# Second attention: early scores ahead of the turned maxima, wider ones products, and the second copy of the maxima on GpSimd

## The chip, the cores and the metric

The kernel runs on one core of one Trainium2 chip. The metric is the device time of one execution in microseconds (us), taken as the median of several runs. The engines are TensorE (PE, its weight loads are shown apart as PEld), VectorE (DVE), ScalarE (ACT), GpSimd (POOL) and SyncE (SP), which here only issues transfers.

## The reference, cut to what matters

The program is two transformer layers. The change touches only the attention of the second one: batch 8, sequence 256, 32 heads of 16 dimensions, causal, float32.

```python
x0, x1 = (xr[..., 0], xr[..., 1])           # rotary, pairs of dimensions
o0 = x0 * c - x1 * s
o1 = x0 * s + x1 * c
...
scores = jnp.einsum('bqhd,bkhd->bhqk', q, k) * scale
scores = jnp.where(causal[None, None], scores, jnp.finfo(scores.dtype).min)
probs = jax.nn.softmax(scores, axis=-1)
out = jnp.einsum('bhqk,bkhd->bqhd', probs, v).reshape(b, s, d)
return out @ wo
```

## The kernel before, in words

The work of this attention is cut into 64 units of four heads each (8 per batch). Queries and keys of a unit come from DRAM as stacks of 52 rows: 4 rows for the negated maximum and 3 times 16 rows for a split of each operand into parts. A unit holds four heads as two halves (row groups 0 to 63 and 64 to 127 of the array) by two slots. The 256 queries and 256 keys are two blocks of 128.

For each unit the kernel computes the scores twice. The first time queries are on the partitions (`scores_early` for query block 0, `scores_late` for query block 1, both on top of a causal mask that `put_masks` writes by a product): from these VectorE takes the negated maximum of every query (`maxima`, one reduction per query block). TensorE turns these maxima from columns to rows (`turn_max`), into the front of PSUM bank 0. ScalarE copies the rows into the first four rows of the queries' stack, for the first half (`negated`, L2062), and again for the second half (`negated_again`, L2067). Then TensorE computes the scores a second time, now with keys on the partitions and with the maxima already subtracted, because they are rows of the stack (`shifted_near` for key block 0, `shifted_far` for key block 1). ScalarE takes the exponential (`exponentials`, L2087: 1024 columns, then 512), GpSimd zeroes what the causal mask leaves out in the diagonal blocks (`cut`), and `values` multiplies with the values and with a block of ones, which yields the sums of the rows. The ones products use, for queries of the second block, the sum of both key blocks' probabilities, which GpSimd has added before (`add_blocks`, L2120). VectorE takes the reciprocal of the sums (L2029) and multiplies (L2032), one block of 128 queries of a pair of units in each step. ScalarE and GpSimd split that into two parts for the last product (L2078, L2126).

The engines are programs of their own, written out by hand; semaphores order them. No scheduler moves anything. All run a loop over steps; in step v TensorE turns the maxima of unit v+1, computes the shifted scores of v, the early and late scores of v+2, and the values of v-1. Four slots hold the stacks; SyncE loads a unit's stack into its slot after the shifted scores of the unit four before it (`load_unit`, four transfers). TensorE executes in order, so each wait holds up all that stands behind it.

PSUM places matter for the waits: the early scores (`s0`) lie in the first half of banks 2 and 3, the shifted scores of key block 1 (`t1`) in the second half of the same two banks. The late scores (`s1`) fill banks 0 and 1, so they overwrite the turned maxima in bank 0: `scores_late` has to wait until ScalarE has copied these (`m_out`).

In the last steps of the stage (from `TAIL` on) each engine also does side work for the output projection, for VectorE an extra subtraction per step (L2492).

Of the kernel before, what the change touches and what calls it, by code (L numbers as in the profile page):

```python
# [21 lines left out]
P = 128  # L22
# [1891 lines left out]
def attention1(nc, io, keep, ctx):  # L1914
# [35 lines left out]
    both = [nc.alloc_sbuf_tensor_at(f"f_both{s}", [P, HU, P], F32, offset=keep.both_at + s * HU * P * 4) for s in range(2)]  # L1950
# [14 lines left out]
    m_out = sem("f_m_out")  # L1965
    t_done = sem("f_t_done")
    p_exp = sem("f_p_exp")
    p_cut = sem("f_p_cut")
    p_both = sem("f_p_both")
# [49 lines left out]
    def vector(dve, side):  # L2019
        def maxima(u, first):  # L2020
            for t, sc in ((0, s0), (1, s1)):
                dve.wait_ge(s_done, 4 * u + 2 * t + 2)
                nc.vector.tensor_reduce(neg_max[first][:, t].rearrange("p (e i) -> p e i", e=2), sc, AX, ALU.max, negate=True).then_inc(smax, 1)  # L2023
# [10 lines left out]
        def step(v, slot, at):  # L2034
            if at < U - 2:
                maxima(v + 2, slot % 2)
# [27 lines left out]
    def negated_again(act, u, slot):  # L2064

        act.wait_ge(m_out, 2 * u + 1)
        nc.scalar.activation(q[slot][64:64 + HU], f32(q[slot][0:HU]), ACT.Identity).then_inc(m_out, 1)  # L2067
# [5 lines left out]
    def scalar(act, side):  # L2073
# [16 lines left out]
        def step(v, slot, at):  # L2090
# [4 lines left out]
            if 0 <= at < U - 1:  # L2095
                negated_again(act, v + 1, (slot + 1) % NS)
# [11 lines left out]
    def gpsimd(pool):  # L2108
# [8 lines left out]
        def add_blocks(u, slot):  # L2117

            pool.wait_ge(p_cut, 2 * u + 2)
            nc.gpsimd.tensor_tensor(both[slot % 2][:], prob0[slot % 2][:, :, P:S], prob1[slot % 2][:], ALU.add).then_inc(p_both, 1)  # L2120
# [7 lines left out]
        def step(v, slot, at):  # L2128
            if 0 <= at < U:
                cut(v, slot)  # L2130
                add_blocks(v, slot)
            if 6 <= at and not slot % 2:
                low((v - 6) // 2)
# [20 lines left out]
    def scores_late(pe, u, slot, first=False):  # L2154

        if not first:
            pe.wait_ge(m_out, 2 * u - 1)
# [35 lines left out]
    def tensor(pe, side):  # L2193
# [20 lines left out]
        def values(u, slot):  # L2214
# [11 lines left out]
            pe.wait_ge(p_both, u + 1)  # L2226
            for p, c, cols in ((prob0[par][:, :, 0:P], 0, slice(0, P)), (both[par], 1, slice(P, S))):
# [5 lines left out]
        def step(v, slot, at):  # L2233
            if 0 <= at < U - 1:
                turn_max(pe, v + 1, (slot + 1) % 2, at)
            if 0 <= at < U:
                pe.wait_ge(m_out, 2 * v + 2)
                if at > 0:
# [3 lines left out]
                if at < U - 2:  # L2242
                    put_masks(0, False)
            if 0 <= at < U - 2:
                scores_early(pe, v + 2, (slot + 2) % NS)
# [23 lines left out]
def output1(nc, io, keep, ctx, out):  # L2269
# [76 lines left out]
    zeroed = sem("g_zeroed")  # L2346
    hi_done, lo_done = sem("g_hi_done"), sem("g_lo_done")
# [567 lines left out]
```

## Time and profile before

| | |
|---|---|
| median of 3 runs | 1948.7 us (1943.15, 1949.42, 1948.7) |
| the profiled execution | 1943.6 us, of which the span is 1941.9 us |
| TensorE, VectorE, ScalarE, GpSimd busy | 95%, 78%, 47%, 47% of the span |
| units of the second attention, first and last turned maxima | 1562.2 to 1791.5 us |
| TensorE's clock granted over the whole span | 0.984 |

The profile gives times from the start of the span. The second attention takes about an eighth of it; what is before it (the first attention, its output projection, the first layer's low-rank part, and the second layer's queries, keys and values) and behind it (output projection and the experts) is not touched. In the rows below a line is a group of like instructions; in a timeline its first number is its start, its second how long it lasted until the last one's end, and the bracket says how long the engine had been idle before it, and what released it.

### The profile page before, as it was taken

To read this page: it belongs to the slowest core of one execution; us is meant where nothing else is said; L and a number is where in the kernel's file an instruction comes from. 1 tells how busy PE (TensorE), PEld (TensorE's weight loads), DVE (VectorE), ACT (ScalarE), POOL (GpSimd) and SP (SyncE) were. 2 spreads that over 40 slices of the span, in tenths; PEclk is the share of its full clock that TensorE was granted. 3 is DMA by queue.
4 is the path that set the end of the run, shared out by engine and by line. 5 is a ranking of instruction groups with operands and counts; after the bars stand their busy time and mean duration, and the time that the engine had idled before them with its cause. 6 is when DMAs were issued, how large, how long until landed. Compare 5 with 4: busy or idle time off the path is not lost.

```text
span 1941.9 us, 38168 instructions
## 1 busy us (share of the span) xinstructions
PE 1853.3 (95%) x12760; PEld 1540.6 (79%) x12760; DVE 1506.6 (78%) x2385; ACT 919.5 (47%) x2297; POOL 907.3 (47%) x872
## 2 busy tenths in 40 slices
PE   8999988999999999999999999998999988998997
PEld 3688867888888888888888888886798966666786
DVE  2577747778888888888888888888788658889887
ACT  1233324444444444444444444454555457888433
POOL 0033354444444444444444444354377557888111
PEclk9999998999999999999999999998999989999999
DMA  9577751111111111111111111231277776554121
GB/s 341 168 231 245 249 166 41 50 49 49 49 50 46 43 41 48 49 49 49 49 49 49 44 42 43 93 96 52 87 233 233 219 223 202 168 168 127 39 65 60
DMA packets 201847, 211.39 MB, mean 109 GB/s; under 512 B 19082, under 2 KB 172682, under 8 KB 200748
## 3 DMA queue, kind: packets, MB, share of 16 engines
q1 hardware_dynamic: 200836, 209.53, 34.8%
q8 instruction: 47, 0.77, 0.2%
q10 hardware_dynamic: 936, 0.85, 0.1%
q14 instruction: 28, 0.23, 0.0%
HBM read 128.40 MB, written 73.53 MB: 104 GB/s over the span
## 4 chain that ended last, share of the span: by engine, by line
PE 68%; issue 13%; DVE 10%; POOL 4%; SPq 3%; DMA 2%; ACT 1%; DVEq 0%; POOLq 0%; ACTq 0%
PE ps L1066 18%; PE ps L1027 17%; PE ps L1040 7%; PE ps L1055 5%; PE ps L1078 4%; DVE f_neg_max L2023 4%; PE ps L1050 3%; SPq L1338 2%; POOL k_rot L574 2%; PE ps L2603 2%; PE ps L2639 2%; PE ps L1839 2%; PE ps L2197 2%; PE ps L2176 1%; PE ps L1849 1%
## 5 line engine op out<-in xcount | busy, mean ns | idle before, releaser
L1066 PE MATMUL ps<-wo,ot 128*128 (+1 forms) x1536 | 389.1, 402 | 0.0
L1066 PEld LDWEIGHTS ps<-wo,ot 128*128 128x128 f32 x1536 | 283.1, 191 | 58.8
L821 ACT ACTIVATE prob<-ps,neg_max 128x128 f32<-128x128 f32 (+1 forms) x512 | 208.6, 421 | 131.2 <-DVE neg_max L902 109.2
L1027 PE MATMUL ps<-ht_hi,wq 128*128 (+1 forms) x1024 | 255.5, 392 | 5.5 <-DVE q_swap L895 5.5
L981 POOL TENSOR_TENSOR q_rot<-q_rot,q_swap 128x512 f32<-128x512 f32 x128 | 164.7, 1288 | 180.0 <-DVE q_swap L895 175.4
L828 ACT ACTIVATE pt<-ps 128x512 fp32r<-128x512 f32 x192 | 108.0, 597 | 283.7 <-PE ps L1078 283.6
L1027 PEld LDWEIGHTS ps<-ht_hi,wq 128*128 128x128 f32 x1024 | 193.2, 189 | 47.8 <-issue 5.9
L975 POOL TENSOR_TENSOR prob<-prob,inv_sum 128x512 f32<-128x512 f32 x64 | 66.6, 1041 | 292.2 <-DVE inv_sum L911 292.2
L574 POOL TENSOR_TENSOR k_rot<-k_rot,k_swap 128x512 f32<-128x512 f32 x32 | 60.2, 1883 | 193.7 <-DVE k_swap L479 193.7
L877 DVE TENSOR_TENSOR ot<-ps,ot 128x512 fp32r<-128x512 f32 x128 | 88.3, 691 | 76.6 <-ACT ot L838 76.4
L1040 PE MATMUL ps<-pt,vv 128*128 128x512 f32 x576 | 144.4, 395 | 3.4 <-issue 2.9
L2023 DVE TENSOR_REDUCE f_neg_max<-ps 128x4 f32<-128x512 f32 (+1 forms) x128 | 116.8, 952 | 33.2 <-PE ps L2142 25.5
L1027 PE MATMUL ps<-ht_lo,wq 128*128 (+1 forms) x512 | 137.8, 391 | 0.0
L1040 PEld LDWEIGHTS ps<-pt,vv 128*128 128x128 f32 x576 | 108.9, 190 | 29.2 <-issue 3.8
L838 ACT ACTIVATE ot<-ps 128x512 fp32r<-128x512 f32 x128 | 76.8, 600 | 106.1 <-PE ps L1040 106.1
L872 DVE TENSOR_TENSOR pt<-ps,pt 128x512 fp32r<-128x512 f32 x192 | 120.9, 684 | 6.0 <-ACT pt L828 4.0
L885 DVE TENSOR_TENSOR x_stream<-ps,x_stream 128x512 f32 (+1 forms) x112 | 77.4, 691 | 58.6 <-PE ps L1066 56.3
L2087 ACT ACTIVATE f_prob<-ps 128x1024 f32<-128x1024 f32 (+1 forms) x128 | 102.0, 798 | 28.6 <-DVE f_neg_max L2023 26.5
L1027 PEld LDWEIGHTS ps<-ht_lo,wq 128*128 128x128 f32 x512 | 96.7, 189 | 20.2
L1078 PE MATMUL ps<-ident,prob 128*128 128x128 f32 x768 | 98.5, 279 | 12.9 <-POOL prob L975 11.4
L1078 PEld LDWEIGHTS ps<-ident,prob 128*128 128x128 f32 x768 | 90.1, 144 | 23.0 <-POOL prob L975 12.5
L1055 PE MATMUL ps<-kk,q 128*128 128x256 f32 x768 | 107.4, 289 | 0.0
(247 smaller groups left out, 4125.5 us busy)
## 6 DMA issues: line engine op xcount, KB each, us to landing
stack_dram<-e_part SPq DMA_DIRECT2D x192, 128.0 KB, 2.4
v_dram<-v_part SPq DMA_DIRECT2D x32, 512.0 KB, 5.9
k_dram<-k_part SPq DMA_DIRECT2D x64, 256.0 KB, 2.5
kk<-k_dram SPq DMA_DIRECT2D x128, 128.0 KB, 2.1
vv<-v_dram SPq DMA_DIRECT2D x128, 128.0 KB, 2.1
f_q<-stack_dram SPq DMA_DIRECT2D x124, 104.0 KB
f_k<-stack_dram SPq DMA_DIRECT2D x124, 104.0 KB
wmod<-in_wmod SPq DMA_DIRECT2D x12, 1024.0 KB, 11.9
```

What stands on the lines that cost most here:

```text
L574: nc.gpsimd.tensor_tensor(krot[g % 2][:], krot[g % 2][:], kswap[g % 2][:], ALU.add).then_inc(k_rot, 1)
L821: nc.scalar.activation(p[:, h], sc[:, h], ACT.Exp, bias=neg_max[:, t, h:h + 1], accum_out=row_sum[:, t, h:h + 1]).then_inc(p_exp, 1)
L828: nc.scalar.activation(pt[0][:, j], ps_s[:, j], ACT.Identity).then_inc(t_hi, 1)
L872: nc.vector.tensor_tensor(pt[1][:, j], ps_s[:, j], f32(pt[0][:, j]), ALU.subtract).then_inc(t_lo, 1)
L981: nc.gpsimd.tensor_tensor(qrot[:, at, j], qrot[:, at, j], qswap[j][:], ALU.add).then_inc(q_add, 1)
L1027: mm = nc.tensor.matmul(ps_q[j][:], w[:, at:at + HD0], r[:, bass.ds(b, 2), k], start=(n == 0), stop=(n == len(passes) - 1))
L1040: mm = nc.tensor.matmul(ps_o[j][:], a[:, k], p[:, blk], start=(n == 0), stop=(n == len(passes) - 1))
L1055: mm = nc.tensor.matmul(s1[:, h], a[:, slot(r, h // 2), h % 2], b[:], start=(n == 0), stop=(n == 2))
L1066: mm = nc.tensor.matmul(ps_y[j][:], o[:, j, h * P:(h + 1) * P], w[:, bass.ds(at + h * D, D)], start=(n == 0), stop=(n == len(passes) - 1))
L1078: mm = nc.tensor.transpose(ps_s[:, blk, h * P:(h + 1) * P], src, keep.ident[:])
L2023: nc.vector.tensor_reduce(neg_max[first][:, t].rearrange("p (e i) -> p e i", e=2), sc, AX, ALU.max, negate=True).then_inc(smax, 1)
L2087: nc.scalar.activation(p[slot % 2][:].rearrange("p (e i) s -> p e i s", e=2), sc, ACT.Exp, scale=SCALE1).then_inc(p_exp, 1)
```

## The change

Three things are changed. First, on TensorE, in step v the masks and early scores of unit v+2 are moved from behind the shifted scores of v to the very front of the step, ahead of the turned maxima of v+1. They now wait for VectorE's first reduction of unit v+1 and for both exponentials of unit v-1; the mask product now starts its accumulation group. VectorE's reduction of those scores now also waits for the shifted scores of unit v. Second, the ones products stream the probabilities themselves: key block 0 with all 256 queries and key block 1 with the second 128, in place of 128 and 128 columns; GpSimd's addition is gone. Third, the second copy of the maxima is made by GpSimd, ahead of its two cuts, and not by ScalarE behind the exponentials; it has a semaphore of its own, `m_again`, and `m_out` now counts one per unit.

```diff
@@ vector: maxima
-        def maxima(u, first):
+        def maxima(u, first, at):
+            if at >= 0:
+                dve.wait_ge(t_done, 4 * u - 4)
             for t, sc in ((0, s0), (1, s1)):
@@ the second copy, now a function of gpsimd
-        act.wait_ge(m_out, 2 * u + 1)
-        nc.scalar.activation(q[slot][64:64 + HU], f32(q[slot][0:HU]), ACT.Identity).then_inc(m_out, 1)
+            pool.wait_ge(m_out, u + 1)
+            nc.gpsimd.nop(nofuse=True)
+            nc.gpsimd.tensor_copy(q[slot][64:64 + HU], f32(q[slot][0:HU])).then_inc(m_again, 1)
@@ scalar: step
-            if 0 <= at < U - 1:
-                negated_again(act, v + 1, (slot + 1) % NS)
@@ gpsimd
-        def add_blocks(u, slot):
-            pool.wait_ge(p_cut, 2 * u + 2)
-            nc.gpsimd.tensor_tensor(both[slot % 2][:], prob0[slot % 2][:, :, P:S], prob1[slot % 2][:], ALU.add).then_inc(p_both, 1)
...
         def step(v, slot, at):
+            if 0 <= at < U - 1:
+                if at == 0:
+                    pool.wait_ge(keep.row_zeroed, 2)
+                if at >= 1:
+                    pool.wait_ge(p_cut, 2 * v)
+                if at >= 6 and slot % 2:
+                    pool.wait_ge(o_split, (v - 5) // 2)
+                negated_again(v + 1, (slot + 1) % NS)
+                pool.wait_ge(m_again, v + 2)
             if 0 <= at < U:
                 cut(v, slot)
-                add_blocks(v, slot)
@@ tensor: scores_late
-            pe.wait_ge(m_out, 2 * u - 1)
+            pe.wait_ge(m_out, u)
@@ tensor: values
-            pe.wait_ge(p_both, u + 1)
-            for p, c, cols in ((prob0[par][:, :, 0:P], 0, slice(0, P)), (both[par], 1, slice(P, S))):
+            for p, c, cols in ((prob0[par], 0, slice(0, S)), (prob1[par], 1, slice(P, S))):
@@ tensor: step
+            if 0 <= at < U - 2:
+                pe.wait_ge(smax, 2 * v + 3)
+                if at > 0:
+                    pe.wait_ge(p_exp, 2 * v)
+                put_masks(0, True)
+                scores_early(pe, v + 2, (slot + 2) % NS)
             if 0 <= at < U - 1:
                 turn_max(pe, v + 1, (slot + 1) % 2, at)
             if 0 <= at < U:
-                pe.wait_ge(m_out, 2 * v + 2)
-                if at > 0:
+                pe.wait_ge(m_again, v + 1)
+                if at >= U - 2:
                     pe.wait_ge(p_exp, 2 * v)
                 shifted_near(v, slot)
                 shifted_far(v, slot)
-                if at < U - 2:
-                    put_masks(0, False)
-            if 0 <= at < U - 2:
-                scores_early(pe, v + 2, (slot + 2) % NS)
             if 0 <= at < U - 2:
                 scores_late(pe, v + 2, (slot + 2) % NS)
```

How TensorE's order changes in one step is seen in its instructions. Before, one step of TensorE reads as follows: turned maxima (`f_neg_max`), shifted scores (`ps<-f_q,f_k`), mask (`halves_b`), early scores (128 columns), mask, late scores (256 columns), values (`f_v`) and ones (`f_ones`).

```order
L2176 MATMUL ps<-ident,f_neg_max_196 4x128 x2
L2197 MATMUL ps<-f_q_50,f_k_54 128x256 x4
L2197 MATMUL ps<-f_q_50,f_k_54 128x128 x4
L2151 MATMUL ps<-halves_b 128x256 x4
L2142 MATMUL ps<-f_k_56,f_q_52 128x128 x4
L2151 MATMUL ps<-halves_b 128x2x128 x4
L2142 MATMUL ps<-f_k_56,f_q_52 128x256 x4
L2224 MATMUL ps<-f_prob_187,f_v_59 32x256 x4
L2224 MATMUL ps<-f_prob_189,f_v_59 32x128 x4
L2229 MATMUL ps<-f_prob_187,f_ones 32x128 x4
L2229 MATMUL ps<-f_both_191,f_ones 32x128 x4
```

The same step in the changed kernel, from its first instruction to its last:

```order
L2159 MATMUL ps<-halves_b 128x256 x4
L2150 MATMUL ps<-f_k_56,f_q_52 128x128 x4
L2184 MATMUL ps<-ident,f_neg_max_194 4x128 x2
L2205 MATMUL ps<-f_q_50,f_k_54 128x256 x4
L2205 MATMUL ps<-f_q_50,f_k_54 128x128 x4
L2159 MATMUL ps<-halves_b 128x2x128 x4
L2150 MATMUL ps<-f_k_56,f_q_52 128x256 x4
L2232 MATMUL ps<-f_prob_187,f_v_59 32x256 x4
L2232 MATMUL ps<-f_prob_189,f_v_59 32x128 x4
L2236 MATMUL ps<-f_prob_187,f_ones 32x256 x4
L2236 MATMUL ps<-f_prob_189,f_ones 32x128 x4
```

A mask and the early scores have gone from behind the shifted scores to the front; between the turned maxima and the second mask only the shifted scores are left; the first group of ones products has 256 columns in place of 128.

GpSimd, two steps before: two cuts of the probabilities and the addition.

```order
L2114 AFFINE_SELECT f_prob_187<-f_prob_187 128x4x128
L2114 AFFINE_SELECT f_prob_189<-f_prob_189 128x512
L2120 TENSOR_TENSOR f_both_191<-f_prob_187,f_prob_189 128x512
L2114 AFFINE_SELECT f_prob_186<-f_prob_186 128x4x128
L2114 AFFINE_SELECT f_prob_188<-f_prob_188 128x512
L2120 TENSOR_TENSOR f_both_190<-f_prob_186,f_prob_188 128x512
```

The same two steps in the changed kernel:

```order
L2120 CAST f_q_52<-f_q_52 4x512
L2113 AFFINE_SELECT f_prob_187<-f_prob_187 128x4x128
L2113 AFFINE_SELECT f_prob_189<-f_prob_189 128x512
L2120 CAST f_q_53<-f_q_53 4x512
L2113 AFFINE_SELECT f_prob_186<-f_prob_186 128x4x128
L2113 AFFINE_SELECT f_prob_188<-f_prob_188 128x512
```

The copy of the maxima (`CAST`) stands ahead of the cuts, and the additions are gone.

## Rows read from the trace of the kernel before

**Rows 1.** Windows of two stretches: span, busy by engine, clock, DMA share, GB/s

```profile
1589.02:1767.55 178.53, 163.17 (x3020) 119.28 (x3016) 154.01 (x208) 149.61 (x234) 147.57 (x181) 0.99 0.60 180
1771.53:1791.37 19.84, 16.11 (x291) 11.45 (x292) 19.67 (x26) 16.80 (x28) 16.04 (x19) 1.00 0.40 121
```

**Rows 2.** Waits in the first of these stretches: total us, times, longest us

```profile
PEld ps L2176 <- DVE f_neg_max L2023: 25.7, 50, 0.5
DVE f_neg_max L2023 <- PE ps L2142: 13.5, 41, 2.1
...
PEld ps L2142 <- DMA f_k<-stack_dram: 3.5, 2, 1.9
```

**Rows 3.** Chain that ended last between 1600 and 1780 us, by line

```profile
by line: DVE f_neg_max L2023 36.0%; PE ps L2197 15.8%; issue 15.0%; PE ps L2176 9.8%; PE ps L2142 6.2%; PE ps L2151 6.1%; DMA f_k<-stack_dram 5.2%; DVE f_inv_sum L2029 1.9%; DVE g_lo L2492 1.7%; SPq L1905 0.8%; PE ps L2224 0.6%; DVEq L2030 
```

**Rows 4.** Timeline of TensorE's weight loads over one unit: start us, us

```profile
1690.69 0.09 PEld L2176 LDWEIGHTS ps<-ident,f_neg_max 128*4 128x4 f32 x2 [0.51 <-DVE f_neg_max L2023]
1691.00 0.54 PEld L2197 LDWEIGHTS ps<-f_q,f_k 52*128 52x128 f32 x8 [0.22 <-ACT f_q L2067]
1691.52 0.12 PEld L2151 LDWEIGHTS ps<-halves_b 64*128 64x128 bf16 x4
1691.64 0.31 PEld L2142 LDWEIGHTS ps<-f_k,f_q 52*128 52x128 f32 x4
1691.93 0.12 PEld L2151 LDWEIGHTS ps<-halves_b 64*128 64x128 bf16 x4
1692.06 0.30 PEld L2142 LDWEIGHTS ps<-f_k,f_q 52*128 52x128 f32 x4
1692.50 0.59 PEld L2224 LDWEIGHTS ps<-f_prob,f_v 128*32 128x32 f32 x16
1693.07 0.24 PEld L2229 LDWEIGHTS ps<-f_prob,f_ones 128*32 128x32 f32 x8
1693.29 0.24 PEld L2229 LDWEIGHTS ps<-f_both,f_ones 128*32 128x32 f32 x8
1694.04 0.09 PEld L2176 LDWEIGHTS ps<-ident,f_neg_max 128*4 128x4 f32 x2 [0.51 <-DVE f_neg_max L2023]
```

**Rows 5.** The same unit on ScalarE, VectorE and SyncE's queue

```profile
1690.55 0.95 DVE L2029 RECIPROCAL f_inv_sum<-ps 128x128 f32<-128x128 f32 x1
...
1691.11 0.59 ACT L2062 ACTIVATE f_q<-ps 4x512 fp32r<-4x512 f32 x1 [0.32 <-PE ps L2176]
...
1691.60 1.00 ACT L2087 ACTIVATE f_prob<-ps 128x1024 f32<-128x1024 f32 x1
...
1691.65 0.29 DVE L2032 TENSOR_TENSOR turned_raw<-ps,f_inv_sum 128x128 f32 x1
...
1692.16 1.82 DVE L2023 TENSOR_REDUCE f_neg_max<-ps 128x4 f32<-128x512 f32 x2 [0.22 <-PE ps L2142]
...
1693.14 0.74 SPq L1905 DMA_DIRECT2D f_k<-stack_dram  x2
```

**Rows 6.** Weight loads at two places where the profile names no releaser

```profile
1575.78 0.09 PEld L2176 LDWEIGHTS ps<-ident,f_neg_max 128*4 128x4 f32 x2 [0.20 <-issue]
1576.10 0.53 PEld L2197 LDWEIGHTS ps<-f_q,f_k 52*128 52x128 f32 x8 [0.22 <-issue]
...
1796.05 0.24 PEld L2229 LDWEIGHTS ps<-f_both,f_ones 128*32 128x32 f32 x8
1796.48 0.53 PEld L2197 LDWEIGHTS ps<-f_q,f_k 52*128 52x128 f32 x8 [0.20 <-issue]
```

**Rows 7.** A place where the second mask does wait for ScalarE's first copy

```profile
1768.58 0.57 ACT L2062 ACTIVATE f_q<-ps 4x512 fp32r<-4x512 f32 x1
...
1769.20 0.11 PEld L2151 LDWEIGHTS ps<-halves_b 64*128 64x128 bf16 x4 [0.40 <-ACT f_q L2062]
```

**Rows 8.** GpSimd's groups: count | busy us, mean ns | idle before

```profile
L2120 POOL TENSOR_TENSOR f_both<-f_prob,f_prob 128x512 f32<-128x512 f32 x64 | 82.1, 1283 | 5.3
L2114 POOL TENSOR_SCALAR_AFFINE_SELECT f_prob<-f_prob 128x512 f32<-128x512 f32 x128 | 81.2, 636 | 44.5 <-ACT f_prob L2087 42.9
```

More of the change, by code:

```diff
@@ L1949, in attention1 @@
     prob1 = [over(f"f_prob1{s}", [P, HU, P]) for s in range(2)]
-    both = [nc.alloc_sbuf_tensor_at(f"f_both{s}", [P, HU, P], F32, offset=keep.both_at + s * HU * P * 4) for s in range(2)]
     inv_sum = [over(f"f_inv_sum{i}", [P, S]) for i in range(2)]
@@ L1965, in attention1 @@
     m_out = sem("f_m_out")
+    m_again = sem("f_m_again")
     t_done = sem("f_t_done")
@@ L1968, in attention1 @@
     p_cut = sem("f_p_cut")
-    p_both = sem("f_p_both")
     o_hi = sem("f_o_hi")
@@ L2035, in step @@
             if at < U - 2:
-                maxima(v + 2, slot % 2)
+                maxima(v + 2, slot % 2, at)
             if 3 <= at and slot % 2:
@@ L2064, in negated_again @@
     def negated_again(act, u, slot):
-        act.wait_ge(m_out, 2 * u + 1)
-        nc.scalar.activation(q[slot][64:64 + HU], f32(q[slot][0:HU]), ACT.Identity).then_inc(m_out, 1)
+        act.wait_ge(m_out, u + 1)
+        nc.scalar.activation(q[slot][64:64 + HU], f32(q[slot][0:HU]), ACT.Identity).then_inc(m_again, 1)
     def scalar_begin(act):
@@ L2115, in cut, with negated_again @@
                                         base=0, channel_multiplier=-1).then_inc(p_cut, 1)
-        def add_blocks(u, slot):
-            pool.wait_ge(p_cut, 2 * u + 2)
-            nc.gpsimd.tensor_tensor(both[slot % 2][:], prob0[slot % 2][:, :, P:S], prob1[slot % 2][:], ALU.add).then_inc(p_both, 1)
+        def negated_again(u, slot):
+            pool.wait_ge(m_out, u + 1)
+            nc.gpsimd.nop(nofuse=True)
+            nc.gpsimd.tensor_copy(q[slot][64:64 + HU], f32(q[slot][0:HU])).then_inc(m_again, 1)
         def low(w):
@@ L2346, in output1 @@
     zeroed = sem("g_zeroed")
+    keep.row_zeroed = zeroed
     hi_done, lo_done = sem("g_hi_done"), sem("g_lo_done")
```

## The prediction

> **What bounds the kernel now.** Only the second attention is touched, so I read first the windows over its even part [rows 1]. From the turned maxima at 1589.02 to those at 1767.55 there are 52 units in 178.53 us. TensorE is busy for 163.17 of it and VectorE for 154.01: nothing is saturated, so a loop through several engines must set the pace. The five units from 1771.53 to 1791.37 take 19.84 / 5 = 3.97 us each, and there VectorE is busy for 19.67 of 19.84 us.
>
> Then the waits [rows 2]: in 50 of those 52 units TensorE's turned maxima wait for VectorE's reduction, 25.7 / 50 = 0.51 us of idle weight loader each time, and VectorE's reduction in turn waits for the early scores (13.5 us in 41 units). The chain of waits names the same ring [rows 3]: reduction 36%, shifted scores 16%, turned maxima 10%, early scores and masks 6% each. The ring is: second reduction, turned maxima, shifted scores, mask, early scores, first reduction, second reduction.
>
> How long TensorE itself needs comes from the starts of its weight loads over one unit [rows 4]. Turned maxima to shifted scores 0.31; to the first mask 0.52; to the early scores 0.12; to the second mask 0.29; to the late scores 0.13; to the values 0.44; to the first ones group 0.57; to the second ones group 0.22; from there 0.75 to the next turned maxima, which includes the wait. Without a wait that last step is 0.43 us, as where shifted scores follow the ones at once (1796.05 to 1796.48, [rows 6]). So TensorE needs 2.60 + 0.43 = 3.03 us of a period of 1694.04 - 1690.69 = 3.35 us, and waits for 0.32. VectorE needs 1.74 us for the two reductions up to the next reciprocal (it starts one period, 3.35 us, after 1690.55 [rows 5], at 1693.90, and the reductions at 1692.16), 1691.65 - 1690.55 = 1.10 to its multiplication and 0.29 for that: 3.13 us.
>
> **Masks and early scores in front of the turned maxima.** Their 0.12 + 0.29 = 0.41 us leave the ring. The first reduction still waits for the shifted scores (its new wait), so it could start 0.41 us earlier; but VectorE is then free only 0.2 us earlier (the bracket at 1692.16, [rows 5]), and its own 3.13 us become the ring's floor. That part alone would give back at most 0.22 us per unit. Nothing is paid on VectorE by its new wait: the shifted scores end about 0.31 + 0.52 + 0.1 = 0.9 us after the turned maxima start, VectorE's multiplication ends 1691.94 - 1690.69 = 1.25 us after them. Had VectorE slack, the wait would still be over before the second reduction.
>
> The price is on TensorE. The late scores overwrite the turned maxima in bank 0, so the second mask waits for ScalarE's first copy. Until now 0.31 + 0.52 + 0.12 + 0.29 = 1.24 us of work lay between the turned maxima and that mask. Now only 0.31 + 0.52 = 0.83 us does. The copy starts 1691.11 - 1690.69 = 0.42 us after the turned maxima [rows 5], with ScalarE free in time; and where TensorE really waited for it, the mask came 1769.20 - 1768.58 = 0.62 us after the copy's start [rows 7]. So the mask can start at 1.04 us, and TensorE, which executes in order, stands still for 1.04 - 0.83 = 0.21 us in every unit, with the late scores, the values, the ones and the next unit's masks behind it. The cover of the copy was just the work that is moved away.
>
> Moving also changes neighbours. The ones are followed by a mask in place of the turned maxima: 0.43 us as before [rows 6], since that row too goes from a 128 by 32 to a half-array shape. The early scores are followed by the turned maxima, a change to another shape. No row shows this pair. The bounds are 0.29 (early scores to mask, same shape) and 0.44 (late scores to values, a change of shape, but with twice the columns) [rows 4]; I take the middle, 0.37.
>
> The Trainium skill, in "TensorE: Matmul & The Clock Gate", section "Step-by-step: what each phase is for", says that the array pulls weight loads ahead of running matmuls where row groups don't conflict or the background buffer is free. By that rule alone the change of neighbours would cost nothing and this pair would be at 0.29 us, 4 us less over the 52 units. The row at 1796.48 speaks for a cost: with nothing to wait for, the loader was idle for 0.20 us at a change of shape [rows 6].
>
> **Ones products.** Their first group goes from 128 to 256 columns, the second stays at 128. Both groups of 128 columns start 0.22 us apart [rows 4], so 128 columns more cost 0.22 us. It is not hidden if TensorE is the bound. The ones no longer wait for the addition, but the row at 1693.07 shows no wait for it [rows 4], so nothing is gained there.
>
> **Sum for one unit on TensorE.** From turned maxima to second mask 1.04; to late scores 0.13; values 0.44; ones 0.57; ones groups 0.44 + 0.43; mask to early scores 0.12; early scores to turned maxima 0.37. Together 3.54 us, against 3.35 now: 0.19 us more. With both bounds for the unknown pair it is 3.46 to 3.61. VectorE's 3.13 and everything else lie below it, so TensorE becomes the bound, and VectorE's reduction is done before the turned maxima ask for it.
>
> **Second copy on GpSimd.** ScalarE loses a copy that the profile names as what released the shifted scores, after 0.22 us of idle weight loader [rows 4]. Where it names nothing the loader pauses for the same 0.22 us, and the shifted scores stand 0.32 us behind the turned maxima just so [rows 6]: it is the passage between the shapes, and the copy held nothing up. GpSimd loses an addition of 1.28 us and gains a copy of 512 elements per partition in four partitions. The trace has no such copy. Its nearest rows are the cut, 0.64, and the addition, 1.28 [rows 8]; I take 0.64. GpSimd's work was 147.57 / 52 = 2.84 us per unit [rows 1]; with a copy of even 1.28 in place of the addition it stays 2.84, in a period of 3.54. The copy starts about 1.04 us after the turned maxima, before the first exponential ends (1692.60, 1.91 us after them [rows 5]), so it does not delay the cuts; and it is needed only in the next step, some 2 us later. Both edges: 0, with up to 0.4 us later cuts, which have over a microsecond of slack until the values one step on.
>
> **The other places.** Five units are bound by VectorE with its side work at 3.97 us [rows 1] and stay so, since 3.54 is less: 0. The other seven units pay the 0.22 us of the ones, 1.5 us. Loads: the early scores now need the stack earlier in the step: they began 1691.64 - 1690.69 = 0.95 us after the turned maxima [rows 4] and now begin 0.37 ahead of them, 1.32 us, of which two longer periods give back 0.38: 0.94 us. Keys came late already, in two units by the weight loader's waits (3.5 us together, 1.9 at the longest, [rows 2]). Each late unit, and one or two more that were nearly late, could lose 0.94, or nothing where the next waits less: 0 to 3, I take 1.
>
> **The sum.** 52 x 0.19 = 9.9, and 1.5, and 1: 12.4 us more. Against the profiled execution's 1943.6 us that is 1956.0. The median of the runs shown is 5.1 us above the profiled execution; against it, it is 1961, which I give.
>
> **Rivals.** First, the ring's gain wins, and the kernel is faster. The place is the wait of the second mask: if the first copy were done within 0.83 us after the turned maxima, or the mask did not have to wait, TensorE would need 3.54 - 0.21 = 3.33, and with the pair at 0.29 and the passage from ones to mask as smooth as from shifted scores to mask (0.2 less) 3.05, so that VectorE's 3.13 decides: 52 x -0.22 = -11 us, 1937. For it speaks that TensorE and VectorE both show idle time which this order fills, and that TensorE's ends are modelled. Against it: the copy's own 0.59 us. It decides below 3.24 us per unit (-5.8 us). Halfway, at 3.18, it gives -9 us: 1940. Chance 0.12.
>
> Second, it cancels: both unknown passages at their low ends (pair 0.29, ones to mask 0.33) give 3.36, nothing: 1950 with the ends. For it speaks that masks load in 0.12 us and were reached from shifted scores without a gap. Chance 0.17.
>
> Third, the loads become the bound. From the keys' issue (done at 1693.14 + 0.74 = 1693.88 [rows 5]) to the early scores two steps on (1691.64 + 6.70 = 1698.34) there were 4.5 us; now there are 3.5. The share of the DMA engines is 0.60 already [rows 1]. When loads land is not in the rows; should it be 4.0 us behind the issue, each pair of units waits 0.5 us: 26 x 0.5 = 13 on top, 1974. Against it: with 4.5 us only two units made TensorE wait. Chance 0.07.
>
> **How the numbers follow.** The forecast, 3.46 to 3.61 us per unit, gets 0.64; it gives 52 x 0.11 + 1.5 = 7 to 52 x 0.26 + 4.5 = 18 us more, 1956 to 1967. Within 0.3% (5.8 us) a measurement can't be told from no change. Faster by more: 0.10 (the first rival nearly whole). Same: 0.21 (the second, and the low edge of the forecast). Slower: 0.69. The range runs from 1944, which leaves out most of the first rival, to 1971, which leaves out the third.
>
> **What would show it.** Per unit about 3.54 us between turned maxima; the second mask with a wait of about 0.2 us for ScalarE's L2063 in nearly every unit; no more waits of the turned maxima for VectorE, and 0.3 to 0.4 us of idle VectorE per unit, waiting for the late scores or shifted scores; ones groups 0.44 us apart; a GpSimd copy of about 0.64 us. Wrong it would be if the mask showed no wait, if turned maxima still waited for VectorE at a period near 3.15, or if the keys' loads released TensorE in most units.

## The result, and the profile after

The changed kernel is slower, as forecast: 1953.4 us against 1945.8 us in the median of seven runs each (1951.6 to 1956.6, and 1942.6 to 1949.4). The ratio is 1.0044, 95% interval 1.0030 to 1.0057. By the ratio that is 8.6 us more (the two medians are 7.6 us apart), where 12.4 us were forecast. The profiled execution took 1952.3 us against 1943.6, 8.7 us more; the sums below are made against it.

The windows over the same two stretches (columns as in [rows 1]) are, for the changed kernel:

```profile
1588.03:1778.13 190.10, 183.64 (x3018) 122.87 (x3016) 155.37 (x207) 115.78 (x184) 112.71 (x181) 0.99 0.57 170
1778.13:1799.00 20.87, 20.42 (x342) 13.67 (x341) 20.66 (x31) 16.29 (x27) 12.78 (x21) 1.00 0.45 132
```

The first line is again 52 units. They take 190.10 us in place of 178.53, and TensorE is now busy for 183.64 of them, 97%, where it was 91%. The second line is the last six units, 20.87 us. In the kernel before, the last six took 1791.36 - 1767.55 = 23.81 us.

The waits in the first stretch (total us, times, longest us), which answer to [rows 2]:

```profile
ACT f_q L2063 <- PE ps L2184: 76.3, 52, 3.4
...
DVE f_neg_max L2024 <- PE ps L2205: 25.8, 52, 2.6
...
PEld ps L2205 <- issue: 11.6, 52, 0.2
PEld ps L2159 <- ACT f_q L2063: 11.1, 52, 0.2
PEld ps L2159 <- DVE f_neg_max L2024: 10.1, 51, 0.2
...
PEld ps L2150 <- DMA f_k<-stack_dram: 3.5, 3, 2.2
```

The wait of the turned maxima for VectorE is gone from the list. In its place the second mask waits for ScalarE's first copy in 52 of 52 units, 11.1 / 52 = 0.21 us each, and VectorE waits for the shifted scores in all of them, 25.8 / 52 = 0.50 us each (0.3 to 0.4 forecast); it has the time now. The row with 10.1 us names VectorE for the first mask, 0.20 us each time; in the runs below the same gap stands there with "issue" as its cause, so it is the change of shape, not VectorE.

TensorE's weight loads over one unit of the changed kernel, which answer to [rows 4]:

```profile
1692.70 0.09 PEld L2184 LDWEIGHTS ps<-ident,f_neg_max 128*4 128x4 f32 x2
1693.01 0.53 PEld L2205 LDWEIGHTS ps<-f_q,f_k 52*128 52x128 f32 x8 [0.22 <-issue]
1693.76 0.11 PEld L2159 LDWEIGHTS ps<-halves_b 64*128 64x128 bf16 x4 [0.22 <-ACT f_q L2063]
1693.89 0.30 PEld L2150 LDWEIGHTS ps<-f_k,f_q 52*128 52x128 f32 x4
1694.33 0.59 PEld L2232 LDWEIGHTS ps<-f_prob,f_v 128*32 128x32 f32 x16
1694.90 0.67 PEld L2236 LDWEIGHTS ps<-f_prob,f_ones 128*32 128x32 f32 x16
1695.77 0.11 PEld L2159 LDWEIGHTS ps<-halves_b 64*128 64x128 bf16 x4 [0.20 <-DVE f_neg_max L2024]
1695.89 0.30 PEld L2150 LDWEIGHTS ps<-f_k,f_q 52*128 52x128 f32 x4
1696.26 0.09 PEld L2184 LDWEIGHTS ps<-ident,f_neg_max 128*4 128x4 f32 x2
```

Read as a sum: 0.31 to the shifted scores, 0.75 to the second mask (forecast 0.73 with the wait), 0.13, 0.44, 0.57, 0.87 for the ones and the passage to the mask (forecast 0.87), 0.12, 0.37 from early scores to turned maxima (forecast 0.37). Together 3.56 us; forecast 3.54.

The chain of waits between 1600 and 1780 us, which answers to [rows 3], now holds TensorE, ScalarE's copy and, where they came late, keys; VectorE is gone from it:

```profile
by line: PE ps L2232 20.2%; PE ps L2159 18.3%; PE ps L2236 16.6%; ACT f_q L2063 15.2%; PE ps L2150 11.3%; PE ps L2184 8.6%; DMA f_k<-stack_dram 7.2%; issue 2.1%; SPq L1905 1.3%; PE ps L2205 0.6%
```

GpSimd's copy takes 611 ns, nearer to the cut than to the addition [rows 8] (count | busy us, mean ns | idle before):

```profile
L2120 POOL CAST f_q<-f_q 4x512 fp32r<-4x512 f32 x63 | 38.5, 611 | 78.7 <-ACT f_q L2063 78.7
```

And the place that the forecast missed, VectorE in one of the last units of the changed kernel. A unit of the kernel before, in the same view, is set under it:

```profile
1784.60 0.95 DVE L2030 RECIPROCAL f_inv_sum<-ps 128x128 f32<-128x128 f32 x1
1785.58 0.29 DVE L2033 TENSOR_TENSOR turned_raw<-ps,f_inv_sum 128x128 f32<-128x128 f32 x1
1785.79 0.68 DVE L2502 TENSOR_TENSOR g_lo<-g_raw,g_w 128x512 fp32r<-128x512 f32 x1
```

```profile
1771.40 0.94 DVE L2029 RECIPROCAL f_inv_sum<-ps 128x128 f32<-128x128 f32 x1
1772.37 0.29 DVE L2032 TENSOR_TENSOR turned_raw<-ps,f_inv_sum 128x128 f32<-128x128 f32 x1
1772.58 1.12 DVE L2492 TENSOR_TENSOR g_lo<-g_raw,g_w 128x512 fp32r<-128x512 f32 x1
```

The same subtraction of 512 columns takes 0.68 us and not 1.12. On GpSimd, in the kernel before, the addition lay beside it. The addition kept its usual 1.27 us; the subtraction, which started later, was stretched, and so was GpSimd's next instruction, which started during the subtraction (its normal time is 0.73 us):

```profile
1771.88 1.27 POOL L2120 TENSOR_TENSOR f_both<-f_prob,f_prob 128x512 f32<-128x512 f32 x1
1773.11 1.18 POOL L2126 TENSOR_TENSOR turned_lo<-turned_raw,turned 128x256 fp32r<-128x256 f32 x1
```

Where the 8.7 us are, from the starts of the turned maxima's weight loads: up to unit 5, -1.0; 52 even units, 52 x (3.559 - 3.342) = 11.3; pauses among them, 5.0 against 4.8; last six units, -2.9; from there to the end, +1.1. Of the -2.9, five units give 5 x (3.97 - 3.56) = 2.0, and the very last one, 3.06 in place of 3.97, the other 0.9.

### The profile page after: what moved, and what is told of

It reads as the page before. It is cut to its first block, busy times and chain, and to the rows that moved or that the text cites. A ratio compares the mean times of both kernels' runs of the same rounds, so it can differ in the third digit from the quotient of the medians.

```text
span 1950.6 us, 38304 instructions
## 1 busy us (share of the span) xinstructions
PE 1877.3 (96%) x12760; PEld 1544.8 (79%) x12760; DVE 1504.2 (77%) x2385; ACT 876.6 (45%) x2234; POOL 861.4 (44%) x871
## 4 chain that ended last, share of the span: by engine, by line
PE 73%; issue 11%; DVE 5%; POOL 4%; ACT 3%; SPq 2%; DMA 2%; POOLq 0%; DVEq 0%; ACTq 0%
PE ps L1066 18%; PE ps L1027 17%; PE ps L1040 7%; PE ps L1055 5%; PE ps L1078 4%; PE ps L1050 3%; PE ps L1839 3%; POOL k_rot L574 2%; PE ps L2232 2%; PE ps L2613 2%; PE ps L2159 2%; PE ps L2649 2%; PE ps L2236 2%; ACT f_q L2063 2%; SPq L1338 2%
## 5 line engine op out<-in xcount | busy, mean ns | idle before, releaser
L893 DVE TENSOR_TENSOR q_rot<-ps,qcos 128x512 f32<-128x512 f32 x128 | 87.7, 685 | 24.4 <-PE ps L1027 24.3
```

## The experiments

Each was run beside fresh runs of the kernel before, on the same chip, in five rounds; the ratio is taken between these two. The table splits each profiled execution by the starts of the turned maxima's weight loads. "Period" is the mean over units 21 to 54, "pauses" what the 52 units from the fifth on take beyond 52 periods. The ratio is to the kernel before, with its 95% interval.

| kernel | ratio | period | pauses | last six | rest |
|---|---|---|---|---|---|
| before | 1 | 3.342 | 4.8 | 23.8 | 150.5 |
| changed | 1.0044 (1.0030 to 1.0057) | 3.559 | 5.0 | 20.9 | 151.6 |
| e1_wide_only | 0.9989 (0.9978 to 1.0001) | 3.344 | 3.8 | 21.4 | 150.8 |
| e2_old_order | 0.9987 (0.9975 to 0.9999) | 3.344 | 3.2 | 21.1 | 150.7 |
| e3_order_only | 1.0028 (1.0018 to 1.0039) | 3.369 | 8.3 | 23.5 | 152.7 |
| e4_add_in_tail | 1.0059 (1.0044 to 1.0075) | 3.559 | 5.8 | 25.2 | 152.9 |
| e5_split_copy | 1.0018 (1.0007 to 1.0029) | 3.365 | 7.5 | 20.7 | 152.6 |
| n1_far_first | 1.0031 (1.0021 to 1.0040) | 3.419 | 8.9 | 24.1 | 152.2 |
| n2_far_first_copy | 0.9985 (0.9974 to 0.9995) | 3.291 | 7.9 | 21.1 | 151.9 |
| n4_order_split | 1.0027 (1.0018 to 1.0037) | 3.341 | 10.4 | 23.8 | 151.1 |
| s1_before_spread | 0.9985 (0.9972 to 0.9998) | 3.344 | 0.0 | 23.8 | 151.3 |
| s3_after_spread | 1.0039 (1.0025 to 1.0053) | 3.560 | 0.0 | 21.2 | 151.5 |
| s2_best_spread | 0.9966 (0.9954 to 0.9979) | 3.290 | 0.0 | 21.1 | 153.1 |

### One part at a time: the wider ones

```diff
@@ the kernel before, tensor: values; add_blocks and p_both are gone (not shown)
-            pe.wait_ge(p_both, u + 1)
-            for p, c, cols in ((prob0[par][:, :, 0:P], 0, slice(0, P)), (both[par], 1, slice(P, S))):
+            for p, c, cols in ((prob0[par], 0, slice(0, S)), (prob1[par], 1, slice(P, S))):
```

> The kernel before with one part of the change: the ones products stream both key blocks and GpSimd's addition is gone; order of TensorE and ScalarE's second copy as before. Theory (TensorE's own sum against the ring): TensorE needs 3.03 + 0.22 = 3.25 us per unit, less than the ring's 3.34, so the even stretch stays at 3.34 us. The last six units go from 3.97 to about 3.56 us, because VectorE's side subtraction (two operands in SBUF) takes 0.68 us and not 1.12 once GpSimd's addition is not beside it. Together 2 to 4 us faster than before (ratio 0.998). Rival (the wider ones are paid in full whatever the order): 3.56 us per unit, 9 us slower. Rival for the last units (the subtraction was short in the changed kernel because TensorE set the pace there): subtraction at 1.12, 3.97 us per unit, no gain.

The period stays at 3.344 us: 0.22 us more of TensorE's time cost nothing while the ring set the pace. Its turned maxima still wait for VectorE, 10.0 us in 33 units, 0.30 us each in place of 0.51. The last six units fall by 2.4 us, the subtraction by itself to 716 ns on average (0.68 us in seven of eight, and 0.96 where one of GpSimd's cuts lay beside it). So what the wider ones cost hangs on the order around them: nothing here, 0.22 us per unit in the changed kernel. The saving in the last units comes with the addition that is gone. In the whole time it is 2.1 us by the ratio, at the low edge of the 2 to 4 expected, and the interval just reaches no change.

### The order taken back

```diff
@@ the changed kernel, tensor: step; vector's wait for t_done is gone (not shown)
-            if 0 <= at < U - 2:
-                pe.wait_ge(smax, 2 * v + 3)
-                if at > 0:
-                    pe.wait_ge(p_exp, 2 * v)
-                put_masks(0, True)
-                scores_early(pe, v + 2, (slot + 2) % NS)
...
                 shifted_far(v, slot)
+                if at < U - 2:
+                    put_masks(0, False)
+            if 0 <= at < U - 2:
+                scores_early(pe, v + 2, (slot + 2) % NS)
```

> The changed kernel with masks and early scores back behind the shifted scores (and without VectorE's extra wait); wide ones and GpSimd's copy stay. Theory: the order alone brought the wait for ScalarE's first copy (0.21 us) and the extra change of shape (0.08 us), so the period is the ring's 3.34 us, no wait of the second mask, and the last units 3.56: 2 to 4 us faster than before, 11 to 13 faster than the changed kernel. Rival (GpSimd's copy is what costs, by way of the shifted scores' wait for it): shifted scores wait for GpSimd's copy and the period stays over 3.45.

3.344 us, and 11 us faster than the changed kernel by the ratios (0.9987 against 1.0044). Nothing waits for GpSimd's copy: the shifted scores show the same 0.22 us of idle loader in every unit as before, with "issue" as the cause. The copy's place is free.

### The order alone

```diff
@@ the kernel before, tensor: step; the old places of masks and early scores, and vector's wait, as in the change (not shown)
+            if 0 <= at < U - 2:
+                pe.wait_ge(smax, 2 * v + 3)
+                if at > 0:
+                    pe.wait_ge(p_exp, 2 * v)
+                put_masks(0, True)
+                scores_early(pe, v + 2, (slot + 2) % NS)
```

> The kernel before with one part of the change: masks and early scores in front of the turned maxima, VectorE's extra wait; narrow ones with GpSimd's addition and ScalarE's second copy stay. Theory: the second mask waits 0.21 us for ScalarE's first copy in every unit; TensorE needs 3.56 - 0.22 = 3.34 us, by chance the period of before, so the even stretch stays at 3.34 and the last units at 3.97: within 2 us of before. Rival (the shorter ring pays once the ones are narrow): VectorE's 3.13 to 3.2 us per unit, 7 to 11 us faster. Rival (the order is worse by more than its wait): over 3.4.

The weight loads of one unit of this kernel:

```profile
1704.75 0.09 PEld L2178 LDWEIGHTS ps<-ident,f_neg_max 128*4 128x4 f32 x2
1705.06 0.54 PEld L2199 LDWEIGHTS ps<-f_q,f_k 52*128 52x128 f32 x8 [0.22 <-issue]
1705.81 0.11 PEld L2153 LDWEIGHTS ps<-halves_b 64*128 64x128 bf16 x4 [0.21 <-ACT f_q L2064]
...
1707.16 0.24 PEld L2231 LDWEIGHTS ps<-f_both,f_ones 128*32 128x32 f32 x8
1707.60 0.11 PEld L2153 LDWEIGHTS ps<-halves_b 64*128 64x128 bf16 x4 [0.20 <-issue]
1707.72 0.30 PEld L2144 LDWEIGHTS ps<-f_k,f_q 52*128 52x128 f32 x4
1708.10 0.09 PEld L2178 LDWEIGHTS ps<-ident,f_neg_max 128*4 128x4 f32 x2
```

3.35 us, with the wait of 0.21 us in it: TensorE's sum without the wider ones, as expected. The shorter ring gives nothing, since the order that shortens it also takes the cover from the copy. Two things were not expected. Every fourth unit is 3.44 us, which makes the mean 3.369; every pass of the loop holds four units, so it comes once a pass. In that unit VectorE's first reduction starts 1.44 us after the turned maxima and not 1.15; the second exponential, which waits for the reduction, starts at 2.16 and not 1.87, and the mask in front of the next unit waits for the exponential. In the changed kernel the reduction is late by 0.08 us only, and TensorE doesn't wait for it. What delays the reduction was not found out. And the pauses grew from 4.8 to 8.3 us: the early scores wait for late keys twice, as before, but for 5.3 us in total and not 3.5. This is the "0 to 3, I take 1" of the forecast. I had said within 2 us; it is 1.0028, 5 us: missed.

### GpSimd's addition put back in the last units

```diff
@@ the changed kernel, gpsimd: step
                 cut(v, slot)
+                if at >= TAIL:
+                    add_blocks(v, slot)
...
@@ tensor: values (its ones wait for the addition)
+            if place >= TAIL + 1:
+                pe.wait_ge(p_both, u - TAIL + 1)
```

> The changed kernel with GpSimd's addition of the two blocks put back in the last units only (its result isn't used, the ones stay wide and wait for it). Theory (the addition and VectorE's side subtraction, both with two operands in SBUF, hold each other up): the subtraction goes from 0.68 to about 1.1 us in these units and the period from 3.56 to about 3.97, 2 to 3 us slower than the changed kernel; the even stretch stays at 3.56. Rival (the subtraction was shorter for another reason, such as TensorE's pace or ScalarE's lighter load): it stays at 0.68 and the period at 3.56.

GpSimd also waits for the addition of the unit before ahead of its copy. The period stays at 3.559 and the last six units go from 20.9 to 25.2 us. Two of them on VectorE and GpSimd:

```profile
1788.61 1.28 POOL L2127 TENSOR_TENSOR f_both<-f_prob,f_prob 128x512 f32<-128x512 f32 x1
1788.66 1.77 DVE L2515 TENSOR_TENSOR g_lo<-g_raw,g_w 128x512 fp32r<-128x512 f32 x1
1790.01 0.89 POOL L2122 CAST f_q<-f_q 4x512 fp32r<-4x512 f32 x1
...
1792.57 1.27 POOL L2127 TENSOR_TENSOR f_both<-f_prob,f_prob 128x512 f32<-128x512 f32 x1
...
1793.27 1.12 DVE L2515 TENSOR_TENSOR g_lo<-g_raw,g_w 128x512 fp32r<-128x512 f32 x1
1793.81 1.18 POOL L2133 TENSOR_TENSOR turned_lo<-turned_raw,turned 128x256 fp32r<-128x256 f32 x1
```

The subtraction is back at 1.12 us where it starts 0.70 us into the addition, and 1.77 us where it starts 0.06 us into it. In both it ends 0.54 to 0.55 us after the addition's end, and what follows on GpSimd during the subtraction is stretched in turn: the product to 1.18, the copy to 0.89 from 0.60. The addition itself stays at 1.27 to 1.28. So the one that starts second is held up until near the end of the first. That settles the cause. It also gives the length of the units. In the run with the order taken back the subtraction takes 0.68 us, the last units 3.52, and TensorE waits for VectorE in them; with 0.44 us more that is 3.97, with 1.09 more 4.61, and these two lengths alternate here. TensorE never waited for the addition. I expected 3.97 throughout. GpSimd carries the copy as well here, which the kernel before leaves to ScalarE; that this is what moves the addition to the subtraction's start was not tested.

### ScalarE's first copy split

```diff
@@ the changed kernel, negated; m_out then counts two per unit, and the waits for it follow (not shown)
-        src = max_rows.rearrange("p (o s) -> p o s", o=1).broadcast_to([HU, 2, S])
-        nc.scalar.activation(q[slot][0:HU], src, ACT.Identity).then_inc(m_out, 1)
+        nc.scalar.activation(q[slot][0:HU, 0], max_rows, ACT.Identity).then_inc(m_out, 1)
+        act.wait_ge(m_out, 2 * u + 1)
+        nc.scalar.activation(q[slot][0:HU, 1], f32(q[slot][0:HU, 0]), ACT.Identity).then_inc(m_out, 1)
```

> The changed kernel with ScalarE's first copy split in two: 256 columns from PSUM, which let TensorE go on, then the other 256 from the first ones in SBUF. GpSimd copies after both. Theory (TensorE stands still 0.21 us in each unit for this copy): the part from PSUM takes about 0.4 us in place of 0.59, so the second mask is ready about 0.83 us after the turned maxima and hardly waits; the period falls from 3.56 to 3.35 us, 10 to 11 us faster than the changed kernel, 0 to 3 us faster than the kernel before. Rival (the pace is set elsewhere, for example by the first reduction's wait for the shifted scores or by a gap at the change of shapes that is there in any case): the wait of the mask goes away but the period stays above 3.5.

The weight loads around the second mask:

```profile
1720.76 0.09 PEld L2185 LDWEIGHTS ps<-ident,f_neg_max 128*4 128x4 f32 x2
1721.07 0.54 PEld L2206 LDWEIGHTS ps<-f_q,f_k 52*128 52x128 f32 x8 [0.22 <-issue]
1721.61 0.11 PEld L2160 LDWEIGHTS ps<-halves_b 64*128 64x128 bf16 x4
```

With nothing else changed the wait is gone (0.54 to the mask in place of 0.75) and the period is 3.35, with 3.43 every fourth unit: 0.19 us less. This is the direct price of the wait. The gain against the changed kernel is 5 us by the ratios and not 10 to 11, because the pauses grew by 2.5 us and the rest by 1.0; and it is not 0 to 3 us faster than the kernel before, but 3.5 slower.

### Other orders

```diff
@@ the kernel before, tensor: step; the first exponential waits for both
-                shifted_near(v, slot)
                 shifted_far(v, slot)
                 if at < U - 2:
                     put_masks(0, False)
             if 0 <= at < U - 2:
                 scores_early(pe, v + 2, (slot + 2) % NS)
+            if 0 <= at < U:
+                shifted_near(v, slot)
```

> The kernel before with another order only: turned maxima, shifted scores of key block 1 (far), mask, early scores, shifted scores of key block 0 (near), mask, late scores, values, ones. The first exponential waits for both. Theory (the ring of the kernel before passes through all that stands between the turned maxima and the early scores): the near scores, 0.26 to 0.3 us, leave the ring, and the 1.24 us of cover for ScalarE's copy stay. The ring is then 3.05 us, below VectorE's 3.13; but the exponentials start 0.4 us later, and ScalarE's second copy behind them ends about 3.5 us after the turned maxima, which the next far scores want at 3.13 + 0.31: period 3.2 to 3.3 us, last units 3.97: 3 to 8 us faster than before. Rival (ScalarE's chain becomes the bound in full): 3.35 or more, no gain.

This missed: 3.42 us and slower. The rival holds, ScalarE's chain. Between 1640 and 1750 us the waits are:

```profile
ACT f_prob L2087 <- PE ps L2197: 15.7, 32, 0.6
...
PEld ps L2176 <- DVE f_neg_max L2023: 12.5, 32, 0.4
PEld ps L2197 <- ACT f_q L2067: 12.0, 32, 0.4
```

The exponentials start later, the second copy behind them too, and the far scores wait for it 12.0 / 32 = 0.38 us, which is 0.16 more than the passage takes by itself. The turned maxima still wait for VectorE, 0.39 us each: the ring is there too, with the late copy in it.

The next run puts this order into the changed kernel, without VectorE's extra wait.

> The same order with the other two parts of the change: wide ones without GpSimd's addition, and GpSimd's second copy of the maxima. Theory: TensorE's own sum of 3.03 + 0.22 = 3.25 us is the bound, since ScalarE is free of the second copy; last units 3.5 us: 52 x 0.09 + 6 x 0.45 = 7 to 8 us faster than before, 15 to 16 faster than the changed kernel. Rival (VectorE's waits or the loads, asked for earlier, eat it): 3.34, as far as the run with the old order went, 2.5 us faster than before.

With the wider ones and GpSimd's copy, the order works: 3.291 us (forecast 3.25). This is the place where the copy on GpSimd earns something: 3.42 becomes 3.29, though the wider ones, which go in with it, add to TensorE's work. But the gain of 52 x 0.05 = 2.6 us is lost in the pauses (7.9 us), and in all it is 2.9 us faster than the kernel before and not 7 to 8: missed, near its rival. One pause, in windows over a unit with late keys and the next:

```profile
1600.49:1607.88 7.39, 5.13 (x62) 3.19 (x59) 3.87 (x6) 2.14 (x4) 3.15 (x6) 0.77 0.91 283
1607.88:1611.16 3.28, 3.28 (x62) 2.33 (x58) 2.28 (x4) 2.36 (x4) 1.22 (x3) 1.00 0.49 155
```

The first line is 7.39 - 3.29 = 4.1 us longer than a unit. The keys came 2.5 us late; the other 1.6 us come from TensorE's clock, granted at 0.77 on average over this unit, because behind the wait (1604.1 to 1607.4 us) it was 0.50, the lower of its levels, 1.2 and not 2.4 GHz. The 16 products of the values took 1.51 us there in place of 0.86. The DMA engines were busy for 0.91 of the time: a 1 MB weight load of the next stage was under way.

> The order of the changed kernel, narrow ones with GpSimd's addition, ScalarE's second copy, and the first copy split in two as in the run above. Theory: TensorE's sum without the wait is 3.34 - 0.21 = 3.13 us, VectorE's 3.13; ScalarE's copies take 0.15 to 0.2 us more: period 3.13 to 3.25, last units 3.97, less 1 to 4 us for keys that come late: 4 to 8 us faster than before. Rival (ScalarE's chain, longer by the split, holds the shifted scores): 3.34 or more.

The changed order with narrow ones and the split copy comes to 3.30 us, with 3.46 every fourth unit, and 10.4 us of pauses: 1.0027, 5 us slower and not 4 to 8 faster, a miss. ScalarE carries three copies here, and its exponentials start behind two of them. The second exponential ends at 1694.66 us, and the mask in front of the next unit, which waits for it, starts at 1694.78; the loader had then been idle for 0.31 us in place of the 0.20 of the passage. So ScalarE's chain is what holds TensorE, as its rival said, though at this mask and not at the shifted scores. The keys made the weight loads wait for 6.4 us, the most of all these runs.

### The extra loads spread

SyncE's loads of weights, gates and tables for the next stage are cut into thirteen pieces and put one behind every second unit's stack; the wait for a weight matrix counts four pieces.

```diff
@@ sync
-        step(2, True, 1)
-        step(3, True, 3)
-        tables(sp)
-        with sp.Fori(4, U // NS) as n:
+        for n in range(2, 9):
+            step(n, True, pieces)
+        with sp.Fori(9, U // NS) as n:
             step(n, True)
```

> The kernel before with SyncE's extra loads spread: the two 1 MB weight matrices in four pieces each, the gates and nine small tables between the units' stacks, one piece behind every second unit from the eighth to the thirty-fifth. Theory (each pause of the even stretch beyond 3.34 us is a unit's keys that come late behind these loads, and by its low clock afterwards): the pauses, 4.8 us between the turned maxima of units 5 and 57, shrink to under 1.5 us, 3 to 4 us faster than before. Rival (the loads of stacks and values are slow by themselves in this stretch): no change within 1 us.

> The changed kernel with the same spreading. Its pauses beyond 3.56 us were 5.0 us. Theory: they shrink likewise, 3 to 5 us faster than the changed kernel, still 4 to 7 us slower than the kernel before with the same spreading, since the period stays at 3.56. Rival (earlier scores in themselves ask for keys before they can be there): pauses stay over 3 us here though they go away in the kernel before.

> The order with the far scores first, wide ones and GpSimd's copy, with the same spreading. Without it its period was 3.29 us, but two units with late keys cost 8 us. Theory: the 3.29 us stay and the pauses shrink to under 3 us: 4 to 6 us faster than without spreading, 7 to 9 us faster than the kernel before. Rival (shorter periods meet late keys whatever is loaded beside them): pauses stay over 6 us.

In all three the pauses are gone whole from the profiled executions: 0.0 us in 52 units, the changed kernel's too. So the late keys were not the price of early scores as such, but of the extra loads ahead of them in SyncE's queue: the 1 MB loads, or the nine small ones in a row, or both; the runs do not part them. The times gain less than the pauses say. By the ratios the kernel before gains 2.9 us (3 to 4 expected), the far-first one 3.7 (4 to 6 expected). The changed kernel gains 1.0 (3 to 5 expected), and its interval overlaps the one without spreading, so its gain in time is not shown, though the profiled span is 4.7 us shorter. With both kernels free of pauses the changed one is 1.0039 against 0.9985 of the kernel before, 0.5% or 10.5 us slower. That is not the 4 to 7 us expected but 52 times the difference of the periods, 11.3. The last of the three is the fastest kernel of this study: 1935.9 us, ratio 0.9966 (0.9954 to 0.9979), 6.6 us faster than the kernel before and by the ratios 15 us faster than the changed one. TensorE is busy for 171.11 of its 171.11 us:

```profile
1587.24:1758.35 171.11, 171.11 (x3020) 120.62 (x3016) 156.17 (x209) 117.54 (x184) 111.63 (x180) 1.00 0.62 188
1758.35:1779.46 21.11, 20.15 (x352) 13.93 (x348) 20.91 (x31) 16.72 (x29) 15.67 (x23) 1.00 0.45 138
```

The 7 to 9 us expected against the kernel before were just missed: it gives 2.6 us back after the last unit (153.1 against 150.5), which was not looked into.

## Why the prediction was right, and where its size was off

**The bound moves to TensorE.** Right. The period came out at 3.56 (3.54 forecast); TensorE's waits for VectorE disappeared. The period before is 3.342 on average and not the 3.35 of the one unit that was read, so the difference is 0.217 us and not 0.19: 1.4 us more over the 52 units than forecast.

**The copy's cover.** Right, and shown twice: the wait of 0.21 us stands in every unit, and splitting the copy takes it away and 0.19 us of the period with it.

**The unknown passage from early scores to turned maxima.** It measured 0.37. The two bounds were worked out from rows; that their middle was exact is luck. The passage from ones to mask was 0.43 as in [rows 6]. I had read the rule of the Trainium skill on weight loads that are pulled ahead ("TensorE: Matmul & The Clock Gate", "Step-by-step: what each phase is for") as giving 0.29. The trace shows 0.37. The rule has conditions, row groups that don't conflict or the background weight buffer as the target, and no row shows whether they held at this passage; so it is my use of the rule that failed here, and not shown to be the rule.

**Wider ones.** 0.22 us as priced (3.56 us against 3.35 in most units of the order alone, 0.21), and only because TensorE had become the bound: alone they cost nothing.

**GpSimd's copy.** 0.61 us, free, as forecast.

**Late keys.** Forecast 1, measured 0.2 in the profiled execution. It is the least certain term: the pauses run from 3.2 to 10.4 us over the kernels with the same loads, one profiled execution each.

**The other places.** Here a step failed: "Five units are bound by VectorE with its side work at 3.97 us [rows 1] and stay so, since 3.54 is less: 0." They did not stay so. They went to 3.56 us, TensorE's pace, and gave back 2.0 us. I took VectorE's 3.97 us for its own work, when 0.44 us of it was the subtraction held up by the addition that the change removes; without it VectorE's round is 3.52 us, as the run with the order taken back has it. The row was there: 1.12 us for 512 columns, where the same trace has a like subtraction, both operands in SBUF, that starts while GpSimd is idle:

```profile
1797.83 0.68 DVE L2495 TENSOR_TENSOR g_bs<-g_b,g_bs 128x512 fp32r<-128x512 f32 x1
```

The Trainium skill states the mechanism in "SBUF — State Buffer", "Who interferes with whom": a VectorE instruction with two operands in SBUF takes its second through a port that it shares with GpSimd's reads. The runs agree: 1.12 to 1.78 us where it starts during the addition, 0.68 where GpSimd does not read beside its start.

The very last unit, priced at +0.2, gave back another 0.9. Both parts of the change have a share in it: the same interval is 3.50 us with the wider ones alone, 3.83 with the order alone, and 3.06 with both. The five units before the even ones and the one behind the last, priced at 1.3 in all, lie in stretches that came to -1.0 and +1.1, within what these parts vary between the runs (150.5 to 153.1 us after the last unit). So the 3.7 us between 12.4 and 8.7 are several terms: +1.4 for the period, -0.8 for late keys, -3.1 for the last six units (+0.2 priced, -2.9 measured) and -1.2 for the rest. That the sum came as near as it did is in part luck, since terms of both signs cancel.

**VectorE's floor.** The 3.13 us of the forecast are too many. From reciprocal to multiplication they count 1.10 us, which holds idle time; where VectorE sets the pace it is 0.97, and 0.21 from there to its next instruction (1771.40, 1772.37, 1772.58 above). That makes 1.74 + 0.97 + 0.21 = 2.92 us, and the last units with the short subtraction, 3.52 - 0.60, say the same (0.60 is the time from the subtraction's start to the reduction's). No run came down to this floor, and the forecast does not hang on it, only the price of the first rival.

**The base.** I gave 1961 against a median of three runs, 1948.7; of seven runs it is 1945.8. By that base the same sum would have read 1958.

## What to carry to other kernels

Before moving work out of a ring, ask what it was covering: here 0.41 us of masks and scores covered a copy that the second mask must wait for, and TensorE, which takes its products in order, then paid 0.21 us in every unit. Add up the engine that the ring leaves next as a sequence of starts, passages between shapes included; the sum from neighbouring rows was good to 0.02 us of 3.56. And when work is deleted, look at what ran beside it, not only behind it: an instruction that takes longer than a like one elsewhere in the same trace may be held up by a neighbour.

## What the runs showed of the hardware

- VectorE's subtraction of 512 columns with both operands in SBUF and GpSimd's instructions hold each other up, and the one that starts second pays. Beside the addition (1.27 to 1.28 us, not slowed) the subtraction takes 1.12 us when it starts 0.70 us into it and 1.77 when it starts 0.06 us into it, in place of 0.68. Started during the subtraction, GpSimd's product of 256 columns goes from 0.73 to 1.18 us, its copy from 0.60 to as much as 1.08.
- On TensorE the passages from turned maxima (128 by 4) to shifted scores (half array), and from ones (128 by 32) to the mask or to the shifted scores, left the weight loader idle for 0.20 to 0.22 us with nothing to wait for. Not every change of shape costs as much: from early scores to turned maxima it was 0.07 us (1695.89 + 0.30 to 1696.26), from late scores to values 0.14.
- A wait of 2.5 us for keys cost 4.1, since TensorE's granted clock behind it was 0.50 for 3.3 us.
- Nine small transfers in a row held SyncE's queue for 4.4 us (1618.27 to 1622.65 in the kernel before); spread out, they and the weights left no pause.
